# Cross-attention with layer norm on one core: Wo split one slot earlier, and another order of work in the last four slots

## The chip, the cores and the metric
The kernel runs on one core of a Trainium2 chip. The metric is device time in microseconds (us) of that core. Three runs of the kernel before gave 607.12, 606.83 and 604.17, median 606.83.

## The reference
For each of 16 batches, x is 512 rows by 512, the context 77 rows by 512; there are 16 heads of 32 columns:
```
Q = x @ Wq + bq;  K = ctx @ Wk + bk;  V = ctx @ Wv + bv
P = softmax(Q K^T / sqrt(32))            # over the 77 keys, per head
y = (P V) @ Wo + bo + x
out = layer_norm(y) * gamma + beta       # over the 512 columns, eps 1e-5
```
All is in float32. The kernel splits each operand of the large products into a high part and a rest (fp32r) and adds three products: high by high, high by rest, rest by high. It holds x also transposed (x_t).

## The kernel before, in words
`project_context` comes first: K and V of all batches, written to DRAM. Then `attend` runs in **slots**. One slot g is one group of four heads (a chunk c of 128 columns of Q, four chunks a batch), so there are NG = 64 groups, 0 to 63. Every engine goes through the slots in its own program, and each stage of a group stands in a later slot of that program: the scores of a group 3 slots behind its q products (LAG_SCORE), its values (P V) 4 behind (LAG_PV), the output products 8 behind (LAG_OUT), the residual sum 9, the normalisation 10, scaling and store 11. An output tile is 128 rows, four a batch; tiles 0 to 59 (NS = 60) go through the slots, and the last four (60 to 63, the last batch) are made apart by `project_last`. Slots 64 to 67 are the **drain**: no q products are left, and the groups 60 to 63 are "single", taken one by one, where before the values of two groups and their sums stand together. `single`, `at_edge` (slots 1 and 63), `last_batch_chunk` and `last_tile` (slots 64 to 67 are its tiles 0 to 3) say where a slot is. All waits are semaphores written out by hand; the order on an engine is the order in its `slot` function, and behind a wait everything of that engine stands still.

What each engine does, as far as the change touches it:

TensorE (PE). `project_q` (12 products), `values_of_pair` in odd slots, `scores` (L680, four a slot), `rowmax_scores` (L666), `project_out` (L730, four chunks of three products). In the first 8 slots `project_v` (L113) stands in place of the output products. In the drain: two scores, `values` (L691), output chunks 0 and 1, `sums` (L713: the softmax denominators, eight narrow products into den_single, in bank p_v[1]), chunks 2 and 3 with a score behind each. In slots 65 to 67 and after them follows `project_last` (L747): for one chunk c the products of last tiles 0 to 2, nine in number; the last tile's own (t = 3), which need the bank p_s[0], come nine with chunk 2 and three with chunk 3. Output tile 56 (slot 64) is the first of a batch and waits chunk by chunk for ch and cl of groups 56 to 59.

VectorE (DVE). `sum_keys` (L1005, 2.3 us), then behind the sums `invert_sums` (L1013), `spread` (L1023) and `divide` (L1049), which writes cx; `add_residual` (L997), one slot behind the output products of its tile; it frees their bank p_o. After the slots the tail is written out: residuals 58 and 59, the last group's division, then `add_last` (L1127), `center_scale` (L1142) and `divide_shift` (L1150) of the last tiles.

ScalarE (ACT). `exp` (L803), `ctx_high` (L828, the high part ch of cx), `square` (L834), `normalize` (L882), x's high parts (L810), and, on its DMA queue, residual loads (L863), x loads and in slots 1 and 63 `copy_low` (L857: four copies of ql into z, each of which the next instruction of ScalarE stands behind), `load_last` (L877).

GpSimd (POOL). x's rest (L1195), `ctx_low` (L1216, cl), `scale` and `shift` (L1207, L1211: gamma, beta), `add_bo` (L1223), `inverse_std` (L1201), `add_bo_last` (L1227).

SyncE (SP). Loads of K, V and z (the score operand: two copies of qh and one of ql for a pair of groups, L580, and the row maxima, L575), and stores (L613).

**Wo** is loaded raw by SyncE (L567) at the end of slot WO_SLOTS[0] - 1 into four places that later hold something else (cx of both parities, rden, vb), split by ScalarE (L893) and GpSimd (L1256), two chunks a slot, in the slots WO_SLOTS. VectorE may write cx and rden only behind that (`wo_low`): spread and divide of group 0 (slot 5) behind two chunks, divide of group 1 (slot 6) behind all four.

Of the kernel before, what the change touches and what calls it, by code (L numbers as in the profile page):

```python
# [29 lines left out]
DK = 32  # L30
# [17 lines left out]
WO_SLOTS = (4, 5)  # L48
# [312 lines left out]
def attend(nc, block, a, keep, kh_dram, kl_dram, v_dram, out, B, S, S2):  # L361
# [21 lines left out]
    with ExitStack() as ctx:  # L383
# [70 lines left out]
        gamma_tail, beta_tail = p_s[1], p_v[1]  # L454
# [21 lines left out]
        den_single = p_v[1][:, 0:QB]  # L476
# [42 lines left out]
        def _(sp):  # L519
# [63 lines left out]
            def slot(g):  # L583
# [10 lines left out]
                if g.k % 2 == 1 and g.back(1).valid(NG):  # L594
# [5 lines left out]
                    if at_edge(g):  # L600
                        load_maxima(c)
                    else:
                        all_at_least(sp, (ql_ready, c.over(1, 2)))
                        load_z(2, i, ql)
                if g.back(LAG_STORE).valid(NS):
                    store(g.back(LAG_STORE))
# [22 lines left out]
        def _(pe):  # L629
# [53 lines left out]
            def values(g):  # L683
# [4 lines left out]
                bank = p_v[0] if single(g) else p_v[g.k % 2]  # L688
# [18 lines left out]
            def sums(g):  # L707

                pe.wait_ge(part_ready, g.over(1, 1))
                pe.wait_ge(cx_ready, NG - LAG_PV)  # L710
                at_least(pe, rec_ready, g.over(1))
                for j in range(HC):
                    last = nc.tensor.matmul(den_single[DK * j:DK * (j + 1), :], sel[:], part[:, g.k % 2, QB * j:QB * (j + 1)],  # L713
# [21 lines left out]
            def project_last(c):  # L735
# [4 lines left out]
                if c >= NCH - 2:  # L740
                    steps += [(QT - 1, kc) for kc in (range(NCH - 1) if c == NCH - 2 else (c,))]
# [20 lines left out]
            def slot(g):  # L762
# [9 lines left out]
                if not g.valid(NG):  # L772
                    pe.wait_ge(cx_ready, v.over(1, -1) if v.over(1) == NG - LAG_PV else v.over(1))
                    values(v)
                for kc in range(KC):
                    if kc == 2 and not g.valid(NG):
                        sums(v)
# [8 lines left out]
                    if g.valid(NG):  # L786
                        rowmax_scores(g, kc)
                c = last_batch_chunk(g, LAG_PV + 1)
# [6 lines left out]
        def _(act):  # L795
# [56 lines left out]
            def copy_low(g):  # L852
# [3 lines left out]
                for j in range(HC):  # L856
# [42 lines left out]
            def slot(g):  # L899
# [8 lines left out]
                if g.back(1).is_first():  # L908
                    copy_low(g)
                if g.k % 2 == 0 and w.valid(NG) and not single(w):  # L910
                    ctx_high(w)
                if s.valid(NG):
                    exp(s, 0)
                    exp(s, 1)
                if m.valid(NS):
# [3 lines left out]
                if g.back(LAG_NORM - 2).valid(NS) and not g.back(ROWS_SLOT - 1).is_first():  # L919
                    load_residual(g.back(LAG_NORM - 2))  # L920
                if s.valid(NG):
                    exp(s, 2)
                    exp(s, 3)
                if g.k % 2 == 1 and w.valid(NG) and not single(w):
# [9 lines left out]
                if at_edge(g) and not g.back(1).is_first():  # L934
                    copy_low(g)
# [7 lines left out]
                if last_tile(g.back(-1)) == 0:  # L943
# [38 lines left out]
        def _(dve):  # L982
# [25 lines left out]
            def invert_sums(g):  # L1008
# [3 lines left out]
                if single(g):  # L1012
                    nc.vector.reciprocal(rec[:, g.k % 2, :], den_single).then_inc(rec_ready, 1)  # L1013
# [337 lines left out]
```

## Time and profile before

| what | value |
|---|---|
| median of the three runs | 606.83 us |
| the profiled execution | 606.88 us, of which its span 605.0 us |
| TensorE busy | 586.3 us, 97% of the span |
| VectorE, GpSimd, ScalarE busy | 476.1, 445.9, 402.1 us |
| granted TensorE clock, mean | 0.993 of full speed |
| chain that ended last | TensorE 92%, GpSimd 3%, others 1% or less each |
| stretch 0 to 40 us | context projection |
| stretch 40 to about 103 us | slots 0 to 7 |
| stretch 557.8 to 592.5 us | slots 64 to 67 |

The busy share is a mean over stages with different limits. Times in the trace count from the start of the span; the profiled execution's own time is 1.9 us longer than the span. Windows show each engine's busy time in a stretch; a timeline gives, behind an instruction, its engine's idle time before it and what ended it.

### The profile page before, as it was taken

Reading aid. Unit: us, or ns where it says so; the run is one execution under the profiler, and the core shown is the slowest. Engines: PE = TensorE matmul, PEld = TensorE weight load, DVE = VectorE, ACT = ScalarE, POOL = GpSimd, SP = SyncE. Lnnn points to the kernel's source line nnn. Section 1 sums busy time; section 2 is a strip of 40 time slices with the busy share of each in tenths; the row PEclk is TensorE's granted clock in tenths of the full one; section 3 lists DMA queues with packets and bytes.
Section 4 is the critical chain, followed back from the end, with each engine's and each line's share of the span. In section 5 each row is a group of like instructions: output and inputs, shape, how many; then the busy total and the mean of one; then the engine's idle time right before and its main releaser. Section 6 shows DMA issues by size and latency. Waiting matters only on the chain.

```text
span 605.0 us, 10107 instructions
## 1 busy us (share of the span) xinstructions
PE 586.3 (97%) x3102; PEld 426.8 (71%) x3102; DVE 476.1 (79%) x775; ACT 402.1 (66%) x837; POOL 445.9 (74%) x396
## 2 busy tenths in 40 slices
PE   8999989999999999999999999999999999999793
PEld 5877856777777777777777777777777777776462
DVE  5535568888888888888888888888888888888676
ACT  5622444577777777777777777777777777667462
POOL 1364253468888888888888898888888888798785
PEclk9999999999999999999999999999999999999898
DMA  7958996989898888989888889889988989896513
GB/s 272 356 206 226 228 241 173 252 195 228 213 226 218 212 222 219 229 213 235 224 211 216 223 215 222 218 211 228 213 226 222 221 224 225 216 226 156 131 56 136
DMA packets 93476, 129.83 MB, mean 215 GB/s; under 512 B 50000, under 2 KB 50000, under 8 KB 93424
## 3 DMA queue, kind: packets, MB, share of 16 engines
q1 hardware_dynamic: 73888, 93.27, 62.0%
q10 hardware_dynamic: 19536, 35.92, 21.5%
q8 instruction: 25, 0.41, 0.3%
q14 instruction: 27, 0.22, 0.1%
HBM read 53.94 MB, written 24.35 MB: 129 GB/s over the span
## 4 chain that ended last, share of the span: by engine, by line
PE 92%; POOL 3%; ACT 1%; DVE 1%; issue 1%; DMA 1%; ACTq 1%; DVEq 0%; SPq 0%; POOLq 0%
PE p_q L642 28%; PE p_o L730 28%; PE p_s L680 10%; PE p_v L691 10%; PE p_a L666 6%; PE pk L323 5%; PE p_o L113 3%; PE pvv L113 1%; DMA cx<-in_ctx_t 1%; PE p_a L747 1%; POOL prob L1189 1%; PE p_q L747 0%; POOL xl L1195 0%; POOL wol L1256 0%; ACTq L857 0%
## 5 line engine op out<-in xcount | busy, mean ns | idle before, releaser
L803 ACT ACTIVATE prob<-p_s 77x512 f32<-77x512 f32 x256 | 142.0, 591 | 77.0 <-PE p_s L680 70.9
L1064 DVE TENSOR_REDUCE nm<-p_a 128x4 f32<-128x308 f32 x256 | 117.9, 469 | 53.8 <-PE p_a L666 50.3
L1195 POOL TENSOR_TENSOR xl<-xt,xh 128x512 fp32r<-128x512 f32 x60 | 77.3, 1290 | 97.6 <-ACT xh L810 97.5
L1005 DVE TRANSPOSE_TENSOR_REDUCE part<-prob 96x64 f32<-96x2048 f32 x64 | 146.7, 2292 | 0.2 <-ACT prob L803 0.2
L642 PE MATMUL p_q<-xl,wqh 128*128 128x512 f32 x256 | 101.1, 395 | 0.0
L642 PE MATMUL p_q<-xh,wqh 128*128 128x512 f32 x256 | 101.1, 395 | 0.0
L642 PE MATMUL p_q<-xh,wql 128*128 128x512 f32 x256 | 101.0, 394 | 0.0
L730 PE MATMUL p_o<-woh,ch 128*128 128x512 f32 x240 | 96.4, 402 | 1.5 <-DVE y L997 1.2
L680 PE MATMUL p_s<-z,ks 97*77 97x512 f32 x256 | 93.1, 403 | 3.3 <-ACT prob L803 1.7
L730 PE MATMUL p_o<-wol,ch 128*128 128x512 f32 x240 | 95.4, 398 | 0.0
L730 PE MATMUL p_o<-woh,cl 128*128 128x512 f32 x240 | 95.2, 397 | 0.0
L818 ACT ACTIVATE qh<-p_q,bq_col 128x512 fp32r<-128x512 f32 x64 | 44.0, 688 | 76.2 <-PE p_q L642 76.2
L1216 POOL TENSOR_TENSOR cl<-cxt,ch 128x512 fp32r<-128x512 f32 x64 | 82.4, 1303 | 14.4 <-ACT ch L828 14.4
L1223 POOL TENSOR_TENSOR xn<-xn,bo_row 128x512 f32<-128x512 f32 x60 | 77.6, 1293 | 4.1 <-DMA bo_row<-in_bo 2.3
L666 PE MATMUL p_a<-kb,qh 128*128 128x308 f32 x256 | 78.4, 306 | 0.7 <-ACT qh L818 0.3
L1211 POOL TENSOR_TENSOR y<-y,beta_row 128x512 f32<-128x512 f32 x58 | 75.6, 1304 | 4.5
L1207 POOL TENSOR_TENSOR y<-y,gamma_row 128x512 f32<-128x512 f32 x58 | 75.3, 1299 | 0.0
L1056 DVE SCALAR_TENSOR_TENSOR ql<-p_q,bq_col,qh 128x512 fp32r<-128x512 f32 x64 | 47.7, 745 | 33.0 <-ACT qh L818 33.0
L691 PE MATMUL p_v<-prob,vb 77*32 77x512 f32 x512 | 62.0, 599 | 0.0
L666 PEld LDWEIGHTS p_a<-kb,qh 128*128 128x128 f32 x256 | 48.4, 189 | 16.0 <-ACT qh L818 1.3
L730 PEld LDWEIGHTS p_o<-woh,ch 128*128 128x128 f32 x240 | 45.5, 190 | 18.2 <-DVE y L997 3.1
L642 PEld LDWEIGHTS p_q<-xh,wql 128*128 128x128 f32 x256 | 48.1, 188 | 11.5
(140 smaller groups left out, 946.6 us busy)
## 6 DMA issues: line engine op xcount, KB each, us to landing
z<-qh SPq DMA_DIRECT2D x256, 128.0 KB, 3.1
z<-ql SPq DMA_DIRECT2D x120, 128.0 KB, 4.2
xn<-in_x ACTq DMA_DIRECT2D x60, 256.0 KB, 3.7
out_dram<-y SPq DMA_DIRECT2D x60, 256.0 KB, 4.2
xt<-in_x_t ACTq DMA_DIRECT2D x58, 256.0 KB, 4.5
ks<-k_high SPq DMA_DIRECT2D x32, 154.0 KB, 4.5
cx<-in_ctx_t SPq DMA_DIRECT2D x4, 616.0 KB, 5.6
k_high<-kth SPq DMA_DIRECT2D x4, 616.0 KB, 3.6
```

The source lines that it names most:

```text
L642: last = nc.tensor.matmul(p_q[:], w[:, kc, P * c:P * (c + 1)], x[:, i, kc, :], start=(kc == 0 and n == 0), stop=(kc == KC - 1 and n == 2))
L666: nc.tensor.matmul(p_a[t % 2][:, 0:HC * S2], qh[:, g.k // 2 % 2, g.k % 2, P * t:P * (t + 1)], kb[g.k // NCH % 2][:, g.k % NCH, :], start=T ...
L680: nc.tensor.matmul(p_s[j % 2][0:S2, :], ks[0:KR, g.k // NCH % 2, h, :], z[0:KR, i, j, g.k % 2, :], start=True, stop=True).then_inc(s_summe ...
L691: nc.tensor.matmul(bank[DK * j:DK * (j + 1), :], vb[0:S2, g.k // NCH % 2, DK * h:DK * (h + 1)], prob[0:S2, g.k % 2, j, :], start=True, sto ...
L730: last = nc.tensor.matmul(p_o[:], x[:, i, kc, P * t:P * (t + 1)], w[:, kc, :], start=(kc == 0 and n == 0), stop=(kc == KC - 1 and n == 2))
L803: nc.scalar.activation(prob[0:S2, g.k % 2, j, :], p_s[j % 2][0:S2, :], ACT.Exp, scale=SCALE).then_inc(prob_ready, 1)
L1005: nc.vector.tensor_reduce(part[:, g.k % 2, :], prob[0:KP, g.k % 2, :, :].rearrange("p h (i r) -> p (h i) r", r=DK), AX_X, ALU.add, apply_t ...
L1064: nc.vector.tensor_reduce(nm[:, t, g.k % 2:HALF:2], p_a[t % 2][:, 0:HC * S2].rearrange("p (h k) -> p h k", k=S2), AX_X, ALU.max, negate=Tr ...
L1195: nc.gpsimd.tensor_tensor(xl[:, i, n.k % KC, :], xt[:, n.k % 2, :], xh[:, i, n.k % KC, :].bitcast(F32), ALU.subtract).then_inc(xl_ready, 1)
L1211: nc.gpsimd.tensor_tensor(rows(m), rows(m), beta[:], ALU.add).then_inc(y_done, 1)
L1216: nc.gpsimd.tensor_tensor(cl[:, i, g.k % NCH, :], cx[:, g.k % 2, :], ch[:, i, g.k % NCH, :].bitcast(F32), ALU.subtract).then_inc(cl_ready, 1)
L1223: nc.gpsimd.tensor_tensor(xn[:, m.k % 2, :], xn[:, m.k % 2, :], bo[:], ALU.add).then_inc(xb_ready, 1)
```

## The change
Wo is loaded at the end of slot 2 and split in slots 3 and 4. In the drain the values and the sums of single groups use the banks p_v[0] and p_v[1] in turn, each group's sums going to the bank that its values don't use; TensorE's values also wait for the inversion of the group before, and its sums follow all four output chunks. All twelve products of the last tile come in the last `project_last`, so that the one of chunk 2 has nine and the last 21. VectorE adds the residual in the slot of its tile's output products. ScalarE issues the four ql copies of slot 63 two and two around its square and last exponentials, and takes ctx_high(59) in slot 64 behind the first two exponentials, the square and the residual load. GpSimd adds bo before ctx_low(59) and before scaling. The last x tile is loaded in slot 65 (was 63) and gets bo in slot 66 (was 64). In slot 63 SyncE stores a tile before it loads the maxima.
```
@@ -45,7 +45,7 @@
 LAG_STORE = 11
-WO_SLOTS = (4, 5)
+WO_SLOTS = (3, 4)
 ROWS_SLOT = 8
@@ -451,7 +451,7 @@
-        gamma_tail, beta_tail = p_s[1], p_v[1]
+        gamma_tail, beta_tail = p_s[1], p_v[0]
         x_last = [xt[:, 0, :], xt[:, 1, :], bv_row[:], vb[:, B % 2, :]]
@@ -473,7 +473,7 @@
         den_pair = p_a[0][:, HC * S2:HC * S2 + 2 * QB]
-        den_single = p_v[1][:, 0:QB]
+        den_single = [p_v[1 - k][:, 0:QB] for k in range(2)]
@@ -598,11 +598,13 @@
                     if at_edge(g):
+                        if not g.back(1).is_first():
+                            store(g.back(LAG_STORE))
                         load_maxima(c)
...
                         load_z(2, i, ql)
-                if g.back(LAG_STORE).valid(NS):
+                if g.back(LAG_STORE).valid(NS) and not at_edge(g):
                     store(g.back(LAG_STORE))
@@ -685,7 +687,7 @@
                     pe.wait_ge(vb_in[g.k // NCH % 2], g.over(PAIR, 1, 16))
-                bank = p_v[0] if single(g) else p_v[g.k % 2]
+                bank = p_v[g.k % 2]
                 for j in range(HC):
@@ -707,10 +709,9 @@
                 pe.wait_ge(part_ready, g.over(1, 1))
-                pe.wait_ge(cx_ready, NG - LAG_PV)
-                at_least(pe, rec_ready, g.over(1))
+                pe.wait_ge(cx_ready, g.over(1))
                 for j in range(HC):
-                    last = nc.tensor.matmul(den_single[DK * j:DK * (j + 1), :], sel[:], part[:, g.k % 2, QB * j:QB * (j + 1)],
+                    last = nc.tensor.matmul(den_single[g.k % 2][DK * j:DK * (j + 1), :], sel[:], part[:, g.k % 2, QB * j:QB * (j + 1)],
                                             start=True, stop=True)
@@ -737,8 +738,8 @@
                 steps = [(t, c) for t in range(QT - 1)]
-                if c >= NCH - 2:
-                    steps += [(QT - 1, kc) for kc in (range(NCH - 1) if c == NCH - 2 else (c,))]
+                if c == NCH - 1:
+                    steps += [(QT - 1, kc) for kc in range(NCH)]
                 for t, kc in steps:
@@ -770,11 +771,10 @@
                 if not g.valid(NG):
-                    pe.wait_ge(cx_ready, v.over(1, -1) if v.over(1) == NG - LAG_PV else v.over(1))
+                    pe.wait_ge(cx_ready, v.over(1, -1))
+                    pe.wait_ge(rec_ready, v.over(1))
                     values(v)
                 for kc in range(KC):
-                    if kc == 2 and not g.valid(NG):
-                        sums(v)
                     if o.valid(NS):
@@ -785,6 +785,8 @@
                         rowmax_scores(g, kc)
+                if not g.valid(NG):
+                    sums(v)
                 c = last_batch_chunk(g, LAG_PV + 1)
@@ -849,11 +851,11 @@
-            def copy_low(g):
+            def copy_low(g, heads):
...
                 act.wait_ge(ql_ready, PAIR * g.u + g.k + 1)
-                for j in range(HC):
+                for j in heads:
                     act.dma_start(z[DK * 2:DK * 3, i, j, :, :].bitcast(F32),
@@ -906,21 +908,27 @@
                 if g.back(1).is_first():
-                    copy_low(g)
-                if g.k % 2 == 0 and w.valid(NG) and not single(w):
+                    copy_low(g, range(HC))
+                if g.k % 2 == 0 and w.valid(NG) and not single(w) and g.valid(NG):
                     ctx_high(w)
...
                     exp(s, 1)
+                if at_edge(g) and not g.back(1).is_first():
+                    copy_low(g, range(HC // 2))
                 if m.valid(NS):
...
                     load_residual(g.back(LAG_NORM - 2))
+                if g.k % 2 == 0 and w.valid(NG) and not single(w) and not g.valid(NG):
+                    ctx_high(w)
                 if s.valid(NG):
...
                     exp(s, 3)
+                if at_edge(g) and not g.back(1).is_first():
+                    copy_low(g, range(HC // 2, HC))
                 if g.k % 2 == 1 and w.valid(NG) and not single(w):
@@ -931,8 +939,6 @@
                     split_x_high(Slot(0, KC))
-                if at_edge(g) and not g.back(1).is_first():
-                    copy_low(g)
                 if n.valid(NG):
@@ -940,7 +946,7 @@
                     load_last(t)
-                if last_tile(g.back(-1)) == 0:
+                if last_tile(g) == 1:
                     load_last(QT - 1)
@@ -1010,7 +1016,7 @@
                 if single(g):
-                    nc.vector.reciprocal(rec[:, g.k % 2, :], den_single).then_inc(rec_ready, 1)
+                    nc.vector.reciprocal(rec[:, g.k % 2, :], den_single[g.k % 2]).then_inc(rec_ready, 1)
                 else:
@@ -1046,7 +1052,7 @@
                 at_least(dve, cl_ready, g.over(1, -1))
-                nc.vector.tensor_tensor(cx[:, g.k % 2, :], p_v[0 if single(g) else g.k % 2][:], rden[:], ALU.mult).then_inc(cx_ready, 1)
+                nc.vector.tensor_tensor(cx[:, g.k % 2, :], p_v[g.k % 2][:], rden[:], ALU.mult).then_inc(cx_ready, 1)
@@ -1084,7 +1090,7 @@
                     add_bv(i)
-                if m.valid(NS) and not g.valid(NG):
+                if last_tile(g) == 0:
                     add_residual(m)
@@ -1100,6 +1106,8 @@
                     q_low(g)
+                if not g.valid(NG):
+                    add_residual(g.back(LAG_OUT))
                 if v.valid(NG) and single(v):
@@ -1150,14 +1158,13 @@
-            add_residual(Slot(0, NS - 2))
             sum_keys(Slot(0, NG - 1))
             minus_mean_over_std(Slot(0, NS - 3))
+            add_residual(Slot(0, NS - 1))
             invert_sums(Slot(0, NG - 1))
...
             variance_of_squares(Slot(0, NS - 2))
-            add_residual(Slot(0, NS - 1))
             center_scale(NS - 2, 0)
@@ -1231,12 +1238,14 @@
                     ctx_low(e)
+                if b.valid(NS) and not g.valid(NG):
+                    add_bo(b)
                 if g.k % 2 == 0 and w.valid(NG) and not single(w):
...
                     shift(g.back(LAG_SCALE))
-                if b.valid(NS):
+                if b.valid(NS) and g.valid(NG):
                     add_bo(b)
@@ -1249,7 +1258,7 @@
                     add_bo_last(t)
-                if last_tile(g) == 0:
+                if last_tile(g) == 2:
                     add_bo_last(QT - 1)
...
                     pool.wait_ge(wo_high, kc + 1)
```

## Rows read from the trace of the kernel before

**Rows 1.** Windows of the middle: us, busy us of each engine (instructions), granted clock, DMA share, GB/s.
```profile
300.00:500.00 200.00, 200.00 (x1081) 146.18 (x1080) 168.83 (x270) 149.65 (x322) 169.56 (x148) 1.00 0.89 219
```

**Rows 2.** The chain that ended last, start: at us, us, what.
```profile
63.00 0.47 PE p_s L680 x2
...
86.91 2.52 POOL wol L1256 x2
```

**Rows 3.** Timeline of TensorE, slots 5 and 6; in brackets the idle time before.
```profile
80.35 0.67 PE L680 MATMUL p_s<-z,ks 97*77 97x512 f32 x2 [1.28 <-issue]
...
91.34 0.46 PE L680 MATMUL p_s<-z,ks 97*77 97x512 f32 x1 [1.70 <-ACT prob L803]
```

**Rows 4.** Timeline of SyncE's queue (issues), slots 1 to 4.
```profile
56.30 3.88 SPq L575 DMA_DIRECT2D z<-nmt  x4
...
60.74 1.90 SPq L526 DMA_DIRECT2D kb<-k_high  x4
63.75 5.54 SPq L580 DMA_DIRECT2D z<-qh  x8
...
71.88 0.59 SPq L567 DMA_DIRECT2D cxt<-in_Wo  x1
...
73.95 2.95 SPq L575 DMA_DIRECT2D z<-nmt  x4
```

**Rows 5.** Timeline of VectorE, slot 6.
```profile
89.45 0.69 DVE L1049 TENSOR_TENSOR cxt<-p_v,rden 128x512 f32<-128x512 f32 x1 [2.56 <-POOL wol L1256]
```

**Rows 6.** Windows, slot 3, columns as in rows 1.
```profile
64.00:66.00 2.00, 2.00 (x11) 1.62 (x10) 1.38 (x3) 1.29 (x3) 0.00 (x0) 1.00 0.86 211
```

**Rows 7.** Timeline of TensorE, slots 64 and 65.
```profile
563.06 0.26 PE L713 MATMUL p_v<-part,sel 96*32 96x16 f32 x8 [1.89 <-DVE part L1005]
...
569.21 0.60 PE L730 MATMUL p_o<-woh,ch 128*128 128x512 f32 x1 [1.23 <-DVE y L997]
```

**Rows 8.** Timeline of VectorE, slot 65 and the tail.
```profile
568.46 0.69 DVE L997 SCALAR_TENSOR_TENSOR y<-p_o,xn 128x512 f32<-128x512 f32 x1 [3.29 <-POOL xn L1223]
...
586.92 0.26 DVE L1013 RECIPROCAL rec<-p_v 128x16 f32<-128x16 f32 x1 [1.67 <-PE p_v L713]
...
596.43 0.68 DVE L1127 SCALAR_TENSOR_TENSOR vb<-p_s,vb 128x512 f32<-128x512 f32 x1
```

**Rows 9.** Windows in the drain and tail.
```profile
562.00:563.00 1.00, 0.00 (x0) 0.00 (x0) 1.00 (x2) 0.47 (x1) 0.00 (x0) 1.00 0.91 160
570.00:571.00 1.00, 1.00 (x4) 0.77 (x3) 1.00 (x1) 0.01 (x1) 1.00 (x2) 0.50 0.00 0
600.00:601.00 1.00, 0.00 (x0) 0.00 (x0) 1.00 (x2) 0.00 (x0) 1.00 (x3) 0.59 0.48 182
```

**Rows 10.** The chain that ended last, drain.
```profile
569.21 2.73 PE p_o L730 x6
...
578.14 1.60 PE p_o L730 x6
...
590.55 2.10 PE p_s L747 x9
```

**Rows 11.** Timeline of ScalarE and its queue, slots 63 and 64.
```profile
558.61 2.82 ACTq L857 DMA_DIRECT2D z<-ql  x4
561.47 1.01 ACTq L877 DMA_DIRECT2D vb<-in_x  x1
562.53 0.62 ACT L828 CAST ch<-cxt 128x512 fp32r<-128x512 f32 x1 [3.11 <-issue]
...
565.23 1.25 ACT L803 ACTIVATE prob<-p_s 77x512 f32<-77x512 f32 x2 [0.41 <-ACT xn L834]
```

**Rows 12.** Timeline of GpSimd, slot 64 and the tail.
```profile
563.22 1.30 POOL L1216 TENSOR_TENSOR cl<-cxt,ch 128x512 fp32r<-128x512 f32 x1 [3.72 <-ACT ch L828]
...
589.39 1.30 POOL L1216 TENSOR_TENSOR cl<-cxt,ch 128x512 fp32r<-128x512 f32 x1
```

**Rows 13.** DMA issues: KB each, median us from issue to landing.
```profile
out_dram<-y SPq DMA_DIRECT2D x60, 256.0 KB, 4.2
```

More of the change, by code:

```diff
@@ L600, in slot @@
                     if at_edge(g):
+                        if not g.back(1).is_first():
+                            store(g.back(LAG_STORE))
                         load_maxima(c)
@@ L604, in slot @@
                         load_z(2, i, ql)
-                if g.back(LAG_STORE).valid(NS):
+                if g.back(LAG_STORE).valid(NS) and not at_edge(g):
                     store(g.back(LAG_STORE))
@@ L709, in sums @@
                 pe.wait_ge(part_ready, g.over(1, 1))
-                pe.wait_ge(cx_ready, NG - LAG_PV)
-                at_least(pe, rec_ready, g.over(1))
+                pe.wait_ge(cx_ready, g.over(1))
                 for j in range(HC):
-                    last = nc.tensor.matmul(den_single[DK * j:DK * (j + 1), :], sel[:], part[:, g.k % 2, QB * j:QB * (j + 1)],
+                    last = nc.tensor.matmul(den_single[g.k % 2][DK * j:DK * (j + 1), :], sel[:], part[:, g.k % 2, QB * j:QB * (j + 1)],
                                             start=True, stop=True)
@@ L772, in slot @@
                 if not g.valid(NG):
-                    pe.wait_ge(cx_ready, v.over(1, -1) if v.over(1) == NG - LAG_PV else v.over(1))
+                    pe.wait_ge(cx_ready, v.over(1, -1))
+                    pe.wait_ge(rec_ready, v.over(1))
                     values(v)
                 for kc in range(KC):
-                    if kc == 2 and not g.valid(NG):
-                        sums(v)
                     if o.valid(NS):
@@ L787, in slot @@
                         rowmax_scores(g, kc)
+                if not g.valid(NG):
+                    sums(v)
                 c = last_batch_chunk(g, LAG_PV + 1)
@@ L914, in slot @@
                     exp(s, 1)
+                if at_edge(g) and not g.back(1).is_first():
+                    copy_low(g, range(HC // 2))
                 if m.valid(NS):
@@ L920, in slot @@
                     load_residual(g.back(LAG_NORM - 2))
+                if g.k % 2 == 0 and w.valid(NG) and not single(w) and not g.valid(NG):
+                    ctx_high(w)
                 if s.valid(NG):
@@ L923, in slot @@
                     exp(s, 3)
+                if at_edge(g) and not g.back(1).is_first():
+                    copy_low(g, range(HC // 2, HC))
                 if g.k % 2 == 1 and w.valid(NG) and not single(w):
@@ L942, in slot @@
                     load_last(t)
-                if last_tile(g.back(-1)) == 0:
+                if last_tile(g) == 1:
                     load_last(QT - 1)
@@ L1012, in invert_sums @@
                 if single(g):
-                    nc.vector.reciprocal(rec[:, g.k % 2, :], den_single).then_inc(rec_ready, 1)
+                    nc.vector.reciprocal(rec[:, g.k % 2, :], den_single[g.k % 2]).then_inc(rec_ready, 1)
                 else:
@@ L1086, in slot @@
                     add_bv(i)
-                if m.valid(NS) and not g.valid(NG):
+                if last_tile(g) == 0:
                     add_residual(m)
@@ L1102, in slot @@
                     q_low(g)
+                if not g.valid(NG):
+                    add_residual(g.back(LAG_OUT))
                 if v.valid(NG) and single(v):
@@ L1233, in slot @@
                     ctx_low(e)
+                if b.valid(NS) and not g.valid(NG):
+                    add_bo(b)
                 if g.k % 2 == 0 and w.valid(NG) and not single(w):
```

31 lines of the change are left out of this document (14 added, 17 removed).

## The prediction, made before the changed kernel was run
> **What bounds the kernel now.** I read the windows by stage first. In the long middle TensorE has no idle time at full clock [rows 1], so a microsecond is won only where TensorE waits, at the start (slots 0 to 7) and in the drain (slots 64 to 67 and the tail), and what is won there reaches the end, since everything between is TensorE's own work. Then the chain of waits for the start, where I looked for pieces that are not PE: the scores of slot 5, whose own row says 1.28 us idle, and in slot 6 a chain from the Wo splits on GpSimd [rows 2] over the division and the exponential to TensorE, where the row says 1.70 [rows 3]. Then SyncE's queue, to see what is issued ahead of what [rows 4], and last the drain, engine by engine.
>
> **The start.** The four Wo loads move from behind the z loads of slot 3 to the end of slot 2, behind the K blocks; that is at 60.74 + 1.90 = 62.6 instead of 71.88. They hold SyncE 73.95 - 71.88 = 2.07 us [rows 4]. The z loads of slot 3 started at 63.75, so they now start at 64.7, 0.95 late, and the maxima, which stand last, are issued 2.07 - 0.95 = 1.1 us earlier: their last one leaves at 75.8, not 76.9. The scores of slot 5, the first to need them, started at 80.35, 3.45 us after that, where TensorE was ready at 80.35 - 1.28 = 79.07 [rows 3]. For the pair before, the last maxima left at 56.30 + 3.88 = 60.18 and the scores ran at 63.00 without a wait [rows 2, 4]: 2.8 us are enough, and 75.8 + 2.8 is 78.6. So the whole 1.28 goes; bounds 0 and 1.28 (at 3.45 us of flight it would be 1.1).
> ScalarE and GpSimd split Wo one slot earlier, at the ends of slots 3 and 4. GpSimd's only other work until then is one x split of 1.3 us a slot, so the splits (2.52 us for two, [rows 2]) are hidden; on ScalarE they are two copies at the end of a slot, where it then waits for TensorE's q products; a late landing of Wo would use up that wait first. In slot 6 the division no longer stands behind the splits (it waited 2.56 us, [rows 5]), the copy to ch follows, and the exponential behind it; VectorE is ready 2.5 us earlier, more than TensorE's hole of 1.70, so that goes: 1.7. Start in all: **-3.0**, between -1.7 (slot 5 stays) and -3.2.
> What could eat this: the trace shows the DMA engines at 0.86 of their time at 64 to 66 [rows 6]; Wo's 1 MB comes into that stretch. The rule in the Trainium skill, "DMA: Bandwidth & Descriptors", "Queues, rings and completion order", is that loads of one queue start in the order in which they were issued, and the SP and ACT queues share the same 16 engines; that speaks against the move, for it would put all of Wo's transfer in front of z. By it the scores of slot 5 would gain nothing. It is the rival below.
>
> **The drain, before.** In slot 64 TensorE stands 1.89 us before the sums (VectorE's key sums of slot 60 end late), and in slot 65 1.23 us before the output products, until VectorE has added the residual of tile 56, which waits for GpSimd's bo addition [rows 7, 8]. TensorE's granted clock is still 1.00 (2.4 GHz) in the idle 562 to 563, and 0.50 (1.2 GHz) in 570 to 571 [rows 9]. Six output products take 2.73 us there and 1.60 in slot 66 [rows 10]; these 1.1 us and a third of it more for the three products behind them make about 1.5 us that the low stretch cost.
>
> **The drain, after, step by step at full clock, in the times of the old trace.**
> ScalarE, slot 63: two of the four copies of ql, 2.82 us for four so 1.4 for two, now come before the square and the last two exponentials, two behind them; the load of the last x tile, 1.01, leaves for slot 65 [rows 11]. The last exponentials end 0.6 late (558.2), ctx_high(58) 1.5 late, the normalisation at 561.0. Then come the two exponentials, the square and the residual load of slot 64 (2.1 us, from 563.15 to 565.23 in the old order), and only behind them ctx_high(59): at 563.1 where it was at 562.53. GpSimd: the bo addition, now ahead, fits into the time in which it waits for that copy (3.72 idle there), so it costs nothing; cl(59) takes 1.30 behind ch and ends at 565.1 against 564.5 [rows 12].
> TensorE, slot 64: scores and values 0.3 late; output products 0 to 2 run without the wait for the sums until 562.2; chunk 3 needs cl(59): **one hole of 2.9 us, 562.2 to 565.1**. The sums end the slot at 566.3. VectorE adds residual 56 at once (bo is ready): 566.8 against 569.1, and inverts the sums at 567.1. TensorE needs that for the values of slot 65 (the added wait on rec_ready; behind it stand the output products), at 567.2; the products follow without a wait and end the slot, sums and nine products for the last tiles in, at 574.0. Before, it ended at 576.5. Queued behind the same waits: ctx_high(60) on ScalarE is now at 568.6 and holds back the exponentials of slot 65, which end 0.2 us before TensorE needs them.
> Slot 66: values at 574.5 (inverse at 573.3, set by GpSimd's bo addition at 572.3), end at 581.2; before 583.9. VectorE's add of tile 58 comes one slot sooner and needs the store of tile 54: its shift ends at 574.9, a store lands in 4.2 us at the median [rows 13], so at 579.1; it is wanted at 578.8. With the DMA engines near empty here I cost it 0, bound 0.3.
> Slot 67: values, all twelve output products, then the sums at 585.4; before they came after six, so the chain starts 1.4 us later relative to the slot. On GpSimd the bo addition for the last x tile (1.3) now stands in slot 66 behind ctx_low(62), so the one for tile 59 ends at 586.2, the residual add at 586.9, and only then are the sums inverted. From rec to cl it was 586.92 to 590.69, 3.8 us [rows 8, 12]; now 586.9 to 590.65. TensorE has only nine products (2.1 us, [rows 10]) to cover it, to 587.5: **a second hole of 3.1 us**. The 21 products left take 4.9, to 595.6, and VectorE's last add comes at 595.7 against 596.43 [rows 8]: 0.7 won. Behind it VectorE's list of scale and shift is the same, all instructions of it with the same neighbours.
> Both banks in turn, the moved gamma/beta copies and the store before the maxima in slot 63 are nothing: each stands in time in which its queue waits.
> So the drain at full clock is -0.7, which holds within it that the old low stretch (1.5) is gone.
>
> **The clock.** It will not stay up. The old trace kept 2.4 GHz through 1.89 us of idle time and fell after a stretch with 1.23 us idle and the narrow values products ahead of it; in the tail, where VectorE's add at 596.43 reads the last product [rows 8], it fell only between 600 and 601 [rows 7, 9]. First hole: 2.9 us with little in front and narrow work behind; I take it as a fall, at 1.3 us (of 1.5 in the old trace, since part of it is waiting for VectorE), bounds 0 and 1.6. Second hole: 3.1 us between dense stretches, between the 1.89 which did nothing and the four or more of the tail which did; its price is 0 or 1.6, I take half, 0.8. The Trainium skill ("TensorE: Matmul & The Clock Gate", "HAM oscillation") says too that idle gaps of a kernel with short bursts throw TensorE to half clock again and again; with both holes priced so, the sum is 606.1, that of the first rival.
>
> **Sum.** -3.0 - 0.7 + 1.3 + 0.8 = -1.6, on the profiled execution's 606.88: 605.3. The median shown, 606.83, is the same to 0.05. About 0.5% (3.0 us) is what a measurement of this kernel can tell from no change.
>
> **Rivals.**
> Both holes cost in full. +0.8: 606.1. For it: each hole is longer than any that the old drain has. Against: the second lies between 100% busy stretches. Chance 0.3.
> No fall at all, or one small: -3.0 - 0.7 = -3.7: 603.2. For it: 1.89 us idle did nothing. Chance 0.2.
> Wo in front of z delays z. 1 MB at the 211 GB/s of [rows 6] is 5 us; z of slot 3 is then 3 us later and takes the 1.1 us of slot 5 with it, and keeps a wait of 1.3: 606.4 to 606.9. For it: the order of the queue. Against: the engines have spare time at 64 to 66. Chance 0.1.
> **Slower.** The clock falls in slot 64 and does not come back, since every slot of the drain now has a place where TensorE waits for VectorE's inversion ahead of narrow products (the added rec_ready wait). Place: slots 65 to 67 and the last products; price: one such stretch cost 1.5 in the old trace, and four more like it cost 6. With the start's gain that is 606.9 - 3.7 + 1.3 + 6 = 610.5. It decides when slots 65 and 66 get an idle share like that of slot 64; in my steps they have 0.5 us each. Chance 0.05.
> That the change doesn't do what it says I leave at nothing: each moved call has one place in the code.
> The forecast as summed: 0.35.
>
> **Range and chances.** The likeliest case with its bounds: 603.7 to 606.5. With both-holes and no-fall: **602.8 to 607.3**. Faster by more than 0.5% (below 603.8): the no-fall case and the lower edge of the forecast, 0.28. Slower (above 609.9): 0.05. Same: 0.67.
>
> **What would show it.** Start: Wo issued at 62.6, no wait of VectorE on the Wo split, TensorE's holes at 79 and 90 gone, slot 8 reached 3 us earlier. Drain: one hole before chunk 3 in slot 64, no residual wait in slot 65, a hole of 3 us before the last 21 products; granted clock 0.5 after one or both. I am wrong if the start's holes stay (z landing late), if the drain's slots 65 and 66 have holes of over 1 us, or if the clock's low stretches are none or over two.

## The result, and the profile of the changed kernel

The changed kernel takes 609.05 us (median of 20 runs, 606.56 to 611.38); the kernel before, run beside it, 607.63 (603.78 to 611.61). The medians differ by 1.4 us. The ratio on record, which is not that of the two medians, is 1.0037, 95% interval 1.002 to 1.0054, or 2.2 us slower. That is under the 0.5% bound, though the interval leaves out 1, and the median lies outside the range of 602.8 to 607.3 that was given. Forecast was 1.6 us faster.

The top of the changed kernel's page: span, the busy share of TensorE, and its granted clock in 40 slices. Before, the last slices of the clock read 9898.

```profile
span 607.7 us, 10108 instructions
...
PE 590.4 (97%) x3102; PEld 429.4 (71%) x3102; DVE 476.2 (78%) x775; ACT 402.4 (66%) x837; POOL 445.8 (73%) x396
...
PEclk9999999999999999999999999999999999999697
```

The profiled execution took 609.61 us against 606.88. I cut both traces at the same instructions. From the first q product of slot 0 to the first output product of slot 8 the start went from 65.97 to 64.00 us; from there to the last row-maximum product of slot 63 it is 451.6 and 451.9; from that product to the end of VectorE's last instruction, the drain, it went **from 44.14 to 49.25**. The rest is 0.7 us less before the first q product, where the change has no part: over all profiles of this case that point lies between 39.2 and 40.1 us, whatever the kernel. So -0.7 - 2.0 + 0.3 + 5.1 = +2.7.

The start. SyncE's queue in the changed kernel, the first and last Wo load and the maxima (compare [rows 4]):

```profile
61.52 0.42 SPq L567 DMA_DIRECT2D cxt<-in_Wo  x1
...
62.94 0.43 SPq L567 DMA_DIRECT2D cxt<-in_Wo  x1
...
71.83 2.97 SPq L575 DMA_DIRECT2D z<-nmt  x4
```

Counted from the first q product (40.14 us before, 39.41 now), the first maxima are issued 1.4 us earlier than before, where 1.1 was forecast; the other 0.7 of the two us by the clock of the trace is its earlier start. TensorE's timeline, the scores of slot 5 and then the drain (compare [rows 3, 7]):

```profile
79.54 0.67 PE L682 MATMUL p_s<-z,ks 97*77 97x512 f32 x2 [1.30 <-issue]
...
559.32 0.39 PE L682 MATMUL p_s<-z,ks 97*77 97x512 f32 x1
562.24 0.60 PE L731 MATMUL p_o<-woh,ch 128*128 128x512 f32 x1 [2.53 <-POOL cl L1223]
...
565.45 1.94 PE L693 MATMUL p_v<-prob,vb 77*32 77x512 f32 x8
...
592.42 0.47 PE L748 MATMUL p_q<-woh,ch 128*128 128x512 f32 x1 [2.81 <-POOL cl L1223]
```

The hole of slot 6 is gone; no row of the start but the one at 79.54 has idle time of over 0.4 us. The hole of slot 5 is as long as before, 1.30. The chain of waits goes back to a copy of ql into z that was issued at 71.19, in front of the maxima:

```profile
71.19 7.16 DMA z<-ql
78.35 1.19 issue
79.54 0.67 PE p_s L682 x2
```

That copy landed at 78.35, 0.1 us after TensorE was ready (79.54 - 1.30 = 78.24). The other 1.19 us is "issue", a wait that the view does not name. By the code these scores wait for the copies of qh and ql into z, for the maxima, and for exponentials of the group before, which were long done. The updates of the maxima's semaphore (`mx_in`) stand in the packed trace: the last one came at 79.45, and the scores started 0.09 us behind it; before, it came at 80.26, the scores at 80.35. So in both kernels it is **the landing of the maxima that ends the hole**. Their last load left at 74.80 (71.83 + 2.97) and took 4.65 us; before, it left at 76.90 and took 3.36.

What stands in front of the maxima in the queue is late as well. The time from issue to landing (minimum, median, maximum) of the copies of qh and ql into z between 60 and 82 us, in the changed kernel:

```profile
DMA to landing us min/median/max: 4.7/5.3/7.2
```

and in the kernel before, the same view:

```profile
DMA to landing us min/median/max: 2.3/3.8/4.3
```

In the drain the hole before output chunk 3 of slot 64 ends with GpSimd's cl, as in the prediction, and the second one, before the last 21 products, too. GpSimd's rows for the two, with the bo addition of tile 59 between:

```profile
560.83 1.26 POOL L1223 TENSOR_TENSOR cl<-cxt,ch 128x512 fp32r<-128x512 f32 x1 [1.30 <-ACT ch L830]
...
586.57 1.28 POOL L1230 TENSOR_TENSOR xn<-xn,bo_row 128x512 f32<-128x512 f32 x1
...
591.00 1.27 POOL L1223 TENSOR_TENSOR cl<-cxt,ch 128x512 fp32r<-128x512 f32 x1
```

and VectorE's: the residual of tile 56 (slot 64), that of tile 59, behind that bo addition, and the last add, which waited for the last tile's products (compare [rows 8]):

```profile
563.74 0.69 DVE L1003 SCALAR_TENSOR_TENSOR y<-p_o,xn 128x512 f32<-128x512 f32 x1 [3.01 <-PE p_o L731]
...
587.94 0.69 DVE L1003 SCALAR_TENSOR_TENSOR y<-p_o,xn 128x512 f32<-128x512 f32 x1 [2.34 <-POOL xn L1230]
...
599.15 0.69 DVE L1135 SCALAR_TENSOR_TENSOR vb<-p_s,vb 128x512 f32<-128x512 f32 x1 [2.22 <-PE p_s L748]
```

What the forecast did not have is how long the clock stayed down. Windows of one us, columns as in rows 1, the granted clock third from the end (compare [rows 9]):

```profile
561.00:562.00 1.00, 0.00 (x0) 0.00 (x0) 0.00 (x0) 0.25 (x1) 1.00 (x1) 1.00 0.72 239
562.00:563.00 1.00, 0.76 (x2) 0.66 (x3) 0.00 (x0) 0.00 (x0) 1.00 (x2) 0.71 0.08 15
566.00:567.00 1.00, 1.00 (x8) 0.00 (x0) 1.00 (x3) 0.81 (x2) 0.11 (x1) 0.50 0.24 88
571.00:572.00 1.00, 1.00 (x4) 0.73 (x3) 0.00 (x0) 0.01 (x1) 0.92 (x2) 0.50 0.09 33
573.00:574.00 1.00, 1.00 (x13) 0.70 (x12) 0.90 (x4) 0.59 (x1) 0.00 (x0) 1.00 0.61 233
594.00:595.00 1.00, 1.00 (x4) 0.71 (x4) 1.00 (x4) 0.78 (x2) 1.00 (x2) 0.50 0.00 0
597.00:598.00 1.00, 1.00 (x6) 0.79 (x5) 0.00 (x0) 0.60 (x2) 0.51 (x1) 1.00 1.03 387
```

It is 1.00 in the idle microsecond 561 to 562, falls within the next, and is 0.50 (1.2 GHz) until between 572 and 573: some 10 us, over most of slot 65. Behind the second hole it is 0.50 again from about 593 to 596.6.

### The profile page after: what moved, and what is told of

Its sections match the earlier page's. It is cut to its first block, busy times and chain, and to the rows that moved or that the text cites. A ratio compares the mean times of both kernels' runs of the same rounds, so it can differ in the third digit from the quotient of the medians.

```text
span 607.7 us, 10108 instructions
## 1 busy us (share of the span) xinstructions
PE 590.4 (97%) x3102; PEld 429.4 (71%) x3102; DVE 476.2 (78%) x775; ACT 402.4 (66%) x837; POOL 445.8 (73%) x396
## 4 chain that ended last, share of the span: by engine, by line
PE 88%; SPq 3%; POOL 3%; ACT 1%; DMA 1%; issue 1%; DVE 1%; ACTq 0%; DVEq 0%; POOLq 0%
PE p_o L731 27%; PE p_q L644 27%; PE p_s L682 10%; PE p_v L693 9%; PE p_a L668 5%; PE pk L323 5%; SPq L580 2%; PE p_o L113 1%; DMA z<-ql 1%; PE pvv L113 1%; PE pk L331 1%; PE p_a L748 1%; POOL cl L1223 1%; POOL prob L1196 1%; SPq L575 1%
```

## The experiments

13 kernels ran, four or fewer at a time beside the kernel before on the same chip, 12 runs each (drain_only and combined 6). Each run also lists its mean granted clock. The ratios are of the same kind as above and can differ from those of the medians by up to 0.3%. In the table "slot 5" is TensorE's idle time before the scores of slot 5 in the profile, "drain" the stretch as cut above, with the part of it at low clock up to the last product in brackets, and "clock" the mean over all timed runs.

| kernel | median us | ratio to before (95%) | clock | slot 5 | drain (low) |
|---|---|---|---|---|---|
| before | 605.9 to 606.8 in four sets | 1 | 0.9896 to 0.9912 | 1.28 | 44.1 (3.4) |
| changed | 609.05 | 1.0037 (1.002 to 1.0054) | 0.9871 | 1.30 | 49.3 (13.7) |
| start_only | 606.24 | 0.9986 (0.9962 to 1.001) | 0.9900 | 1.48 | 43.9 (3.4) |
| drain_only | 609.39 | 1.0073 (1.0046 to 1.0101) | 0.9868 | 1.98 | 44.7 (3.4) |
| fill_first | 607.28 | 1.0019 (1.0 to 1.0039) | 0.9908 | 1.12 | 43.8 (0) |
| last_tile_back | 607.78 | 1.0016 (0.9989 to 1.0043) | 0.9874 | 2.53 | 42.1 (0) |
| start_split | 603.35 | 0.9958 (0.9934 to 0.9983) | 0.9918 | 0.54 | 43.6 (3.4) |
| copy_early | 606.0 | 0.9984 (0.9961 to 1.0008) | 0.9903 | 2.22 | 43.5 (3.4) |
| fill_and_last | 605.6 | 0.9967 (0.9941 to 0.9993) | 0.9925 | 0.99 | 42.1 (0) |
| before_filled | 605.84 | 0.9984 (0.9956 to 1.0013) | 0.9930 | 0.77 | 42.9 (0) |
| after_split | 609.81 | 1.0058 (1.0027 to 1.0088) | 0.9847 | 2.81 | 48.1 (10.2) |
| combined | 600.12 | 0.9899 (0.9867 to 0.9932) | 0.9948 | 0 | 40.8 (0) |
| wo_front | 604.12 | 0.9955 (0.9935 to 0.9976) | 0.9928 | 1.98 | 40.8 (0) |
| wo_old | 602.94 | 0.9946 (0.9923 to 0.9969) | 0.9942 | 1.81 | 45.0 (6.8) |
| wo_split | 601.76 | 0.9936 (0.9909 to 0.9963) | 0.9941 | 0 | 41.3 (0) |

Two theories were tested. **C**: the drain's price is the clock, which the holes of slots 64 and 67 throw. **S**: the start's gain is half lost because Wo stands in front of z in the queue, which makes z late. Rivals: the order of waits as such, and chance. S takes the z copies for what TensorE waits for; it is the maxima behind them, as shown above, so its forecasts are to be read with those.

### start_only and drain_only: one half of the change each
The start alone, on the kernel before:
```diff
-WO_SLOTS = (4, 5)
+WO_SLOTS = (3, 4)
```


> The kernel before with Wo loaded in slot 2 and split in slots 3 and 4, drain untouched. Theory S (the start is a gain of which slot 5's half is lost, since Wo stands in front of z in the queue): the hole in slot 6 (1.7 us) is gone, the one before the scores of slot 5 stays at 1.2 to 1.4 us, z loads of slot 3 land in 4.5 to 7 us; 1.5 to 1.8 us faster than before. Rival (the whole start is a loss or nothing on the median, what the profile shows of it being chance): ratio 1.000.

The hole of slot 6 is gone, that of slot 5 is 1.48, z lands in 4.4 to 8.1 us (median 5.5). The median is 0.6 us lower, the interval holds 1: less than the 1.5 to 1.8 that S gave.

The drain alone, the changed kernel with `WO_SLOTS = (4, 5)`:

> The changed kernel with Wo back in slots 4 and 5, so only the drain is changed. Theory C (the hole of slot 64 throws the clock for some 10 us, the one of slot 67 for 3.4): 3.5 to 5 us slower than before, low clock from slot 64 into slot 65. Rival (the drain is level, the start is what made it slower): within 1 us of before.

The ratio says 0.73% slower, 4.4 us; the medians differ by 2.6 us (609.39 against 606.82), from 6 runs. Both are over the rival's 1 us, and start_only is not slower, so the timed runs put the loss into the drain. The profiled run doesn't show it there: its drain is 0.6 us longer than before's, its start 2.1. With a hole of 2.25 us in slot 64 (2.53 in the changed kernel's profile) the clock stayed up, so the same code doesn't always throw it; whether the 0.3 us or chance decides isn't shown. It fell behind the second hole, and in slot 5, behind a hole of 1.98 us. TensorE's timeline row and the window behind it:

```profile
80.12 0.66 PE L682 MATMUL p_s<-z,ks 97*77 97x512 f32 x2 [1.98 <-issue]
...
80.00:82.00 2.00, 1.88 (x6) 1.48 (x7) 0.18 (x1) 1.08 (x2) 0.00 (x0) 0.69 1.16 231
```

That was new: the start has a hole that can throw the clock too.

### fill_first: keep TensorE busy in the first hole
```diff
                 for kc in range(KC):
+                    if kc == KC - 1 and last_tile(g) == 0:
+                        pe.wait_ge(ql_ready, NG)
+                        for _ in range(10):
+                            nc.tensor.matmul(p_q[:], woh[:, 0, 0:P], woh[:, 0, :], start=True, stop=True)
                     if o.valid(NS):
```


> The changed kernel with ten idle-time products (written into p_q, read by nobody, 2.3 us at full clock) in slot 64 ahead of output chunk 3, where TensorE waited 2.5 us. They shorten no wait. Theory C (the price is the clock): granted clock stays 1.00 through slots 64 and 65, slot 65 takes 5 us instead of 9 up to its sums, 3.5 to 4.5 us faster than the changed kernel. Rival (the price is the order of waits: rec_ready and the residual add): no faster, up to 0.3 us slower.

The ten products fill p_q, which nothing reads before its next start. In the profile the low clock of the drain is gone, and the sums of slot 65 come 14.0 us behind the last row-maximum product instead of 17.9. The ratio to before is 1.0019 against the changed kernel's 1.0037, 1.1 us, a third of what C gave (ratios are compared here, since the sets ran apart), and the two intervals overlap, so the timed runs alone show no gain. The profile is the fastest of the 12 runs (603.94), and the second hole is still there. TensorE's row behind it:

```profile
588.31 0.47 PE L748 MATMUL p_q<-woh,ch 128*128 128x512 f32 x1 [2.82 <-POOL cl L1227]
```

and VectorE's rows of the residual of tile 59 and of the last add:

```profile
583.81 0.69 DVE L1007 SCALAR_TENSOR_TENSOR y<-p_o,xn 128x512 f32<-128x512 f32 x1 [2.34 <-POOL xn L1234]
...
593.48 0.69 DVE L1139 SCALAR_TENSOR_TENSOR vb<-p_s,vb 128x512 f32<-128x512 f32 x1 [1.01 <-PE p_s L748]
```

In this run the clock stayed up there as well, so it shows the changed drain at full clock: 43.78 us.

### last_tile_back: the last tile's nine products as cover again
```diff
-                if c == NCH - 1:
-                    steps += [(QT - 1, kc) for kc in range(NCH)]
+                if c >= NCH - 2:
+                    steps += [(QT - 1, kc) for kc in (range(NCH - 1) if c == NCH - 2 else (c,))]
```


> The changed kernel with the last tile's nine products of chunks 0 to 2 back in slot 67, so that 18 products instead of 9 stand before the wait for the last cl, and 12 instead of 21 after it. Theory C: the hole of 2.8 us falls to 0.7, the clock stays up there, and the products behind it are nine fewer: 2.5 to 3.5 us faster than the changed kernel (1.6 clock, 1.1 or more for tile 3 done earlier). Rival (the tail is bound by VectorE's list, not by tile 3): under 1 us.

The hole falls from 2.81 to 0.74 (TensorE's row), and VectorE's last add no longer waits:

```profile
592.05 0.47 PE L748 MATMUL p_q<-woh,ch 128*128 128x512 f32 x1 [0.74 <-POOL cl L1223]
```

```profile
596.12 0.68 DVE L1135 SCALAR_TENSOR_TENSOR vb<-p_s,vb 128x512 f32<-128x512 f32 x1
```

The drain is 42.13 in its profile, 1.65 less than fill_first's at the same full clock. The ratio is 0.0021 under the changed kernel's, 1.3 us, less than expected and inside the noise: the mean clock is as low as there (0.9874). Where it was low in the timed runs isn't known. In the profile it stayed up behind the first hole (2.22 us) and fell for 6.8 us in slot 5, behind a hole of 2.53. fill_and_last has both edits:

> The changed kernel with the ten unread products in slot 64 and with the last tile's nine products back in slot 67. Theory C: effects add up, no low clock in slots 64 to 67 in most runs, drain 42 us instead of 43.8 (ten products alone); median 2 to 3 us under the changed kernel's and 1 to 1.5 under ten products alone. Rival: the last tile's place is hidden by VectorE: same as ten products alone.

The ratio is 0.9967, 0.7% or 4.2 us under the changed kernel's and more than the two parts gave singly (1.1 and 1.3); here the intervals do not overlap. That with one hole mended the other still throws the clock would explain it, but it isn't shown. The rival, the same as with ten products alone (1.0019, 1.0 to 1.0039), is out.

### copy_early: take away the first hole's cause
ScalarE's ctx_high(59) goes back ahead of the exponentials of slot 64, and
```diff
-                if b.valid(NS) and not g.valid(NG):
-                    add_bo(b)
                 if g.k % 2 == 0 and w.valid(NG) and not single(w):
                     ctx_low(w)
+                if b.valid(NS) and not g.valid(NG):
+                    add_bo(b)
```


> The changed kernel with the copy to ch of group 59 back ahead of the exponentials of slot 64, and cl of group 59 ahead of the bo addition. Theory C says the hole before output chunk 3 falls from 2.5 us to under 0.5, and with it both the wait and the low clock: slot 64 2 to 2.5 us shorter, granted clock 1.00 into slot 65, 4 to 6 us faster than the changed kernel in a run in which that fell, about 3 to 4 at the median. Rival (rec_ready and the sums set the slot): a new wait of 2 us before the values of slot 65, under 1 us faster.

The hole falls from 2.53 to 0.51, the second is as it was. A short new wait appears before the scores of slot 65, for the maxima. TensorE's rows with idle time in the drain:

```profile
562.79 0.47 PE L731 MATMUL p_o<-woh,ch 128*128 128x512 f32 x1 [0.51 <-POOL cl L1221]
...
564.57 0.66 PE L682 MATMUL p_s<-z,ks 97*77 97x512 f32 x2 [0.40 <-DMA z<-nmt]
...
588.85 0.47 PE L748 MATMUL p_q<-woh,ch 128*128 128x512 f32 x1 [2.82 <-POOL cl L1221]
```

The ratio is 0.9984 against 1.0037, 3.2 us. So the order in front of cl(59) is what opened the first hole, and the new rec_ready wait and the late sums cost nothing that shows. The new wait is 0.40 us here, but 0.83 in wo_split's profile and 1.55 in wo_old's below.

### before_filled: does the clock cost the kernel before too?
```diff
+                    if kc == 2 and last_tile(g) == 0:
+                        pe.wait_ge(ql_ready, NG)
+                        for _ in range(7):
+                            nc.tensor.matmul(p_q[:], woh[:, 0, 0:P], woh[:, 0, :], start=True, stop=True)
+                    if kc == 0 and last_tile(g) == 1:
+                        for _ in range(5):
+                            nc.tensor.matmul(p_q[:], woh[:, 0, 0:P], woh[:, 0, :], start=True, stop=True)
```


> The kernel before with seven unread products in its hole before the sums of slot 64 and five in the one before the output products of slot 65, both written into p_q. They shorten no wait. Theory C (the clock in the drain costs the kernel before too, about one to two low stretches a run): mean granted clock up by 0.002 to 0.005, 1 to 2 us faster than before. Rival (low clock in before's drain is rare or harmless): no faster.

The clock is higher (0.9930 against 0.9908), the time lower by 0.6, with 1 inside the interval: the direction of C, not a proof of its size. In the profile the clock stays up through the drain, but falls for 3.4 us in slot 6, behind a hole of 1.69 us.

### start_split and after_split: the order in the queue
```diff
-                if g.back(WO_SLOTS[0] - 1).is_first():
-                    for kc in range(KC):
-                        load_wo(kc)
+                for half in range(2):
+                    if g.back(WO_SLOTS[half] - 1).is_first():
+                        for kc in (2 * half, 2 * half + 1):
+                            load_wo(kc)
```


> The kernel before with Wo split in slots 3 and 4, but only its first two chunks loaded in slot 2 and the last two behind the z loads of slot 3. Theory S (the loads in front of z in the queue make z land late, and that holds the hole of slot 5): z lands in 3 to 5 us at the median instead of 5.5, hole of slot 5 down from 1.48 to 0.7 or less, hole of slot 6 gone: 2 to 3 us off the start of before (65.97 us from the first q product to the first output product). Rival (the hole of slot 5 hangs on the moment the maxima are issued, not on what stands in front): hole as in start_only or longer, since the maxima go out no earlier.

On the kernel before, with the splits in slots 3 and 4: the hole of slot 5 is 0.54, the start 63.22 us, the median 3.1 us under before's (2.5 by the ratio). TensorE's row:

```profile
79.35 0.66 PE L681 MATMUL p_s<-z,ks 97*77 97x512 f32 x2 [0.54 <-issue]
```

The same edit on the changed kernel:

> The changed kernel with the last two Wo chunks loaded behind the z loads of slot 3, nothing else. Theory S: start of 63 to 64.5 us from the first q product to the first output product, drain as in the changed kernel, so 1 to 2 us faster than that: 607 to 608 at the median. Rival (the start saved is given back in the drain or hangs on chance): 609.

A miss. 609.81 and a ratio of 1.0058, no faster, and in the profile the hole of slot 5 is 2.81 us; the clock falls behind it, and the start takes 68.25. TensorE's row and two windows:

```profile
80.96 1.11 PE L683 MATMUL p_s<-z,ks 97*77 97x512 f32 x2 [2.81 <-issue]
...
80.00:82.00 2.00, 1.04 (x3) 0.80 (x4) 1.93 (x4) 0.32 (x1) 0.44 (x1) 0.53 1.11 263
...
84.00:86.00 2.00, 2.00 (x7) 1.53 (x6) 0.52 (x2) 0.59 (x1) 0.00 (x0) 0.50 1.03 207
```

The code of the start is the same in both. The hole comes and goes between executions: the last maxima took 3.2 us to land in start_split's profile and 5.7 in this one. The drain's falls hide what it is worth.

### combined, and three places for Wo on it
combined is the changed kernel with the edits of after_split, copy_early and last_tile_back.

> The changed kernel with three parts mended: last two Wo chunks behind the z loads of slot 3; copy to ch and cl of group 59 ahead again; last tile's nine products back in slot 67. Theories S and C together: start 63 to 64, no idle time over 0.8 us in slots 64 to 67, drain of 41 us or less against 44.1 of before in its profile, mean clock above 0.991; 601 to 602.5 at the median, ratio to before 0.991 to 0.994. Rival (one of the waits takes the place of the others): 603.5 to 605.

600.12 us, 1.0% faster than before, from 6 runs: the best of all, and better than forecast. Run again as wo_split below it gave 601.76, 0.6%. Its page's top lines, then TensorE's rows of slot 5 and of the two holes:

```profile
span 598.1 us, 10108 instructions
...
PEclk9999999999999999999999999999999999999998
...
78.36 0.69 PE L683 MATMUL p_s<-z,ks 97*77 97x512 f32 x2
...
559.43 0.47 PE L732 MATMUL p_o<-woh,ch 128*128 128x512 f32 x1 [0.51 <-POOL cl L1222]
...
585.43 0.47 PE L749 MATMUL p_q<-woh,ch 128*128 128x512 f32 x1 [0.71 <-POOL cl L1222]
```

With the drain's two large holes gone the start can be judged. Three kernels, which differ in the place of Wo alone, ran on one chip:

> The combined kernel, but all four Wo loads in slot 2 as in the change, so only the queue's order in the start differs from it. Theory S (Wo in front of z makes z late): hole before the scores of slot 5 of 1 us or more in most runs, 1 to 2 us slower than wo_split at the median. Rival (the hole of slot 5 comes and goes by chance, wherever Wo stands): same as wo_split within 0.7 us.

> The combined kernel with Wo loaded and split where the kernel before did it. Both theories: the hole of slot 6 (1.7 us) is back. Theory S: with it a hole of 1 to 2 us in slot 5, so 2.5 to 4 us slower than wo_split. Rival (chance): 1.7 us slower, no more.

> The combined kernel again, beside the two others on one chip: 599.5 to 601.5 at the median, with now and then a run of 603 to 605, in which the hole of slot 5 is over 2 us and the clock falls there. Rival (its first median was luck): 602.5 or more.

Medians 604.12 (all four loads in slot 2, as in the change), 602.94 (where they were before) and 601.76 (divided, the combined kernel again); means 603.58, 603.50 and 602.48, with 12 runs each. Loading all of Wo in front of z is **not shown to be better than leaving it**, although it removes the 1.7 us of slot 6. Dividing the loads was faster than both, by 1.0 us and more in the means, but the intervals against before overlap, and wo_split's median lies over its forecast (599.5 to 601.5) and under its rival's. wo_old is 1.2 us slower than wo_split where S gave 2.5 to 4 and the rival 1.7: a miss. Its drain was not quiet either: its profile is the slowest of its 12 runs (608.32; the others 602.43 to 604.49), with this row and 6.8 us of low clock behind it:

```profile
566.38 0.71 PE L682 MATMUL p_s<-z,ks 97*77 97x512 f32 x2 [1.55 <-DMA z<-nmt]
```

What the 15 profiles show of slot 5 is the same throughout: wherever there is a hole, the scores start 0.09 us behind the last update of `mx_in`, the landing of the maxima. The last z copy landed before TensorE was ready in all but three (changed, start_only, last_tile_back), and in those less than 0.4 us after it. Times in us, the landing counted from the first q product; TensorE is ready at 38.7 to 39.0 (39.7 in start_only).

| Wo's place | profiles | last maxima landed | from their issue to landing | hole |
|---|---|---|---|---|
| slot 3, behind z (before) | 4 | 39.6 to 40.7 | 2.8 to 4.0 | 0.77 to 1.98 |
| slot 2, in front of z (changed) | 7 | 39.9 to 41.3 | 3.3 to 5.5 | 0.99 to 2.53 |
| divided | 4 | 38.1 to 41.6 | 1.6 to 5.7 | 0 to 2.81 |

So S was right that the gain of slot 5 doesn't come, and wrong on the load that is waited for: with all of Wo in front the maxima leave up to 1.4 us earlier but land no earlier. The spread within a place is as large as the difference between places, so the size of each stays open.

## Why the prediction was wrong, point by point

**The start, -3.0.** The step that failed is "2.8 us are enough, and 75.8 + 2.8 is 78.6. So the whole 1.28 goes". The maxima were the right thing to look at, and they left slightly earlier than worked out; what was wrong is the time until the last of them landed: 4.65 us in the changed kernel and 3.36 before, not 2.8, which was read from the pair before. The working had 3.45 us as a bound, and that was too low as well. The rival with Wo in front of z, to which I gave 0.1, had the order of the queue right and z as the late one; z was late (4.7 to 7.2 us instead of 2.3 to 4.3), but the maxima behind it ended the wait. The rule of the Trainium skill ("DMA: Bandwidth & Descriptors", "Queues, rings and completion order"), that loads of one queue start in the order of their issue, spoke against the move. This trace agrees in that the last copy of ql, the last of the maxima and the K load behind them landed in the order of their issue, at 78.35, 79.45 and 79.92. Slot 6's 1.7 us came as forecast. In the timed runs the start gave 0.6 us, with no change inside the interval (start_only).

**The drain at full clock, -0.7.** This was right to 0.3: fill_first without low clock takes 43.78 against before's 44.14 with its own low stretch, so -0.4. The holes were forecast at 2.9 and 3.1 us and are 2.53 and 2.81 in TensorE's rows; both end with the cl that was named. But the sum hid a choice: beside the same drain with the nine products back (42.13 in last_tile_back, 42.11 in fill_and_last) the edit to the last tile alone loses 1.65 us.

**The clock, +1.3 and +0.8.** Mis-sized, and the largest part of the error. The first fall: the sums of slot 65 come 17.9 us behind the last row-maximum product against 14.0 in fill_first, so 3.9 us, three times the 1.3. The step that failed is the price of "a fall" from the old trace, where dense output products followed at once and the clock was back before 574. Here score and values products of slots 64 and 65 followed, and it stayed at 0.50 for some ten; that their kind is the reason isn't shown. The second: the last 21 products took 6.7 us against 5.1 in fill_first, 1.6, the upper of my two values, not the half. Together 5.5 us where I had 2.1. That is no bad luck of one execution: of the changed kernel's 20 runs 18 have a mean clock of 0.985 to 0.988, and the only two with 0.991 and 0.994 are its fastest, 606.87 and 606.56. An estimate from the means: 0.9871 against 0.9896 to 0.9912 for the sets of the kernel before is 3 to 5 us more at low clock in a run, which costs at most half of that. Where in a run it lies only the profiles show, and of the four with an unfilled first hole of over 2 us the clock fell behind it in two (changed, after_split), behind the second hole of 2.8 us in four of five. The rival "the clock falls in slot 64 and does not come back", held at 0.05 and 610.5, was nearest in number, but by luck: its cause, waits of over 1 us in slots 65 and 66, is not in the trace, which has none over 0.4 there, and the clock did come back.

**The sum.** For the profiled execution: 2.0 for 3.0 at the start and +5.1 for +1.4 in the drain. The error is 1.0 us of start and 3.7 of drain, of which 3.4 is the clock (5.5 for 2.1) and 0.3 the drain at full clock. The range failed since even its case with both falls had them at the old trace's price, and since it left the slot 5 hole as a rival of its own.

## What to carry to other kernels
A hole in TensorE's work has two prices, its own length and that of the clock behind it; in this drain the second was 3.9 us for a hole of 2.53. It cannot be taken from another stretch: the same kernel's older fall was worth 1.5. When the last tile's products are free to move, put them where TensorE would wait, not behind the wait. A load moved ahead in a queue must be priced by when everything behind it lands, not by when it is issued. And when a chain of waits ends in "issue", look up in the code what else the instruction waits for before naming the last piece of the chain as the cause.

## What the runs showed that I had not expected
The clock also falls in the start. In slot 5, where values products and then a wait stand, it did in the five profiles with a hole of 1.98 us or more (drain_only, wo_front, copy_early, last_tile_back, after_split) and not in those with 1.81 or less. That is no bound for other places: in slot 6 it fell behind 1.69 us (before_filled), in the drain behind 1.23 (before) and not behind 2.22 and 2.25 (last_tile_back, drain_only). The length of the hole of slot 5 for the same start ranges from 0 (combined) over 0.54 (start_split) to 2.81 us (after_split). Some of the spread between executions must come from it, how much isn't shown: runs of the combined kernel lie between 599.78 and 606.15. And ten products that nobody reads, put into a hole, raised the mean clock from 0.987 to 0.991 and made the kernel no slower (fill_first).
